# Third graph layer: one wait for landing per sixteen gathers in place of two, and its index copies moved from VectorE to ScalarE

## What is computed

```python
deg_inv_sqrt = where(deg > 0, rsqrt(deg), 0)
norm = deg_inv_sqrt[row] * deg_inv_sqrt[col]        # row, col: edges and self loops
h = x @ weight
out = segment_sum(h[row] * norm[:, None], col, num_segments=n)
return out + bias
```

## Time and profile before

| | us |
|---|---|
| median of 3 executions | 23745.33 |
| lowest and highest of the 3 | 23739.36 to 23776.59 |
| the profiled execution, its own time | 23831.74 |
| its span in the profile | 23829.8 |
| first gather of the third layer's sum, start | 13672.09 |
| last gather of it, start | 16261.36 |

### The profile page before, as it was taken

One profiled execution on the slowest core, in us unless ns is written; L12 is line 12 of the kernel. 1 busy time (PEld: TensorE's weight loads), 2 busy tenths in 40 slices (PEclk: granted clock), 3 DMA queues, 4 the chain that ended last, 5 costly groups with the idle time before them and its releaser, 6 DMA issues. The chain is left out here.

```text
span 23829.8 us, 208218 instructions
## 1 busy us (share of the span) xinstructions
PE 10305.7 (43%) x47565; PEld 6803.8 (29%) x47566; DVE 15503.2 (65%) x25810; ACT 2726.6 (11%) x6634; POOL 12726.1 (53%) x12678
## 2 busy tenths in 40 slices
PE   0033335655555555556666522221433433333333
PEld 0033332222222222222222322221333333333333
DVE  8744439998888888886666211112666666666677
ACT  0011110000000000000000000000222222222222
POOL 0188876666556565536666166663544442544543
PEclk9999995555555555558888555555555555555555
DMA  4033331111111111121111111114222222222222
GB/s 171 23 69 69 69 65 26 24 24 21 23 23 23 21 23 23 23 20 24 24 24 24 7 21 21 21 21 44 54 56 51 54 56 48 52 56 51 57 51 47
DMA packets 1151512, 957.51 MB, mean 40 GB/s; under 512 B 803964, under 2 KB 920316, under 8 KB 1150740
## 3 DMA queue, kind: packets, MB, share of 16 engines
q0 software_dynamic: 419904, 437.84, 11.2%
q1 hardware_dynamic: 730960, 512.22, 8.4%
HBM read 734.68 MB, written 210.63 MB: 40 GB/s over the span
## 5 line engine op out<-in xcount | busy, mean ns | idle before, releaser
L1451 POOL DMA_INDIRECT tail<-ball,h_idx x3328 | 3396.5, 1021 | 3961.9 <-DVEq L1761 1514.0
L737 PE MATMUL p_rad<-w_stack,hid_t 99*128 99x512 bf16 (+1 forms) x6656 | 3077.4, 619 | 2396.3 <-DVEq L827 1117.3
L809 DVE TENSOR_REDUCE red<-prod 128x96 f32<-128x1536 f32 x1664 | 2901.3, 1744 | 3.5
L1487 PE MATMUL h_sum<-head,h_hot 128*128 128x64 f32 x6656 | 1468.1, 422 | 3078.8 <-ACT head L1529 2472.1
L1101 POOL DMA_INDIRECT l_xg<-h_tab,l_idx x1664 | 1573.9, 946 | 1470.0 <-issue 958.3
L1487 PEld LDWEIGHTS h_sum<-head,h_hot 128*128 128x128 f32 x6656 | 1435.4, 332 | 3109.7 <-issue 3109.7
L338 POOL DMA_INDIRECT rec_a<-rec,slot x1600 | 1990.0, 1244 | 517.1 <-issue 510.1
L693 POOL DMA_INDIRECT rec_b<-l_rcb x1600 | 1926.1, 1204 | 570.9 <-issue 514.6
L932 POOL DMA_INDIRECT l_xg<-x_tab,l_idx x1664 | 1574.1, 946 | 1156.7 <-issue 856.8
L948 PE MATMUL l_sum<-outer,l_hot 128*128 128x512 f32 x3328 | 1671.6, 666 | 986.6 <-DVEq L993 904.8
L737 PEld LDWEIGHTS p_rad<-w_stack,hid_t 99*128 99x128 bf16 (+1 forms) x6656 | 773.4, 132 | 4338.8 <-issue 4335.4
(11 more groups left out here) (368 smaller groups left out, 18688.7 us busy)
## 6 DMA issues: line engine op xcount, KB each, us to landing
hot_t<-rows_l SPq DMA_DIRECT2D x208, 512.0 KB
rec_a<-fill SPq DMA_DIRECT2D x128, 728.0 KB, 19.5
l_rec<-rec_a SPq DMA_DIRECT2D x104, 896.0 KB, 4.8
rhot_t<-rows_r SPq DMA_DIRECT2D x208, 384.0 KB
tail<-ball,h_idx POOLq DMA_INDIRECT x3328
t<-in_type SPq DMA_DIRECT2D x100, 500.0 KB
l_xg<-in_x,l_idx POOLq DMA_INDIRECT x1664
l_xg<-x_tab,l_idx POOLq DMA_INDIRECT x1664
```

The source lines that it names most:

```text
L737: ins = pe.matmul(p_rad[j % 2][:, h * 512:(h + 1) * 512], hid_t[j // 4 % 2][0:K3 + 3 * (1 - i), j % 4, i, :], w_stack[i][0:K3 + 3 * (1 - i ...
L809: ch.step(dve.tensor_reduce(red[:, j, :], prod[j % 3][:, :, :], AX, ALU.add))
L1451: pool.indirect_dma_start(tg[q][:, j, :], None, table[:, :], bass.IndirectOffsetOnAxis(ap=idx[q][:, j:j + 1], axis=0)).then_inc(gathered[q ...
L1487: ins = pe.matmul(p_sum[:, j // 2, :], hot[j // HP8 % 2][:, j % HP8, :], hg[:, j, 0:D], start=(j % 2 == 0), stop=(j % 2 == 1))
```

## The change

GpSimd waits once per block, after its sixteenth gather. The index copies of the phase, the four at the start and the one per block, are taken from VectorE and given to ScalarE, which waits for `sum_done` by itself.

```diff
         @block.scalar
         def _(act):
             act.activation(p_row[:, 0:P], g["row"][:, :], ACT.Copy).then_inc(row_ready, 1)
+            for u in range(4):
+                act.activation(idx[u][:, :], g["src_a"][:, u * BT:(u + 1) * BT], ACT.Copy).then_inc(idx_ready, 1)
+            with act.Fori(0, NB // 4 - 1) as it:
+                for u in range(4):
+                    b = it * 4 + u
+                    hold(act, turn, sum_done, b + 1)
+                    act.activation(idx[u][:, :], g["src_a"][:, bass.ds((b + 4) * BT, BT)], ACT.Copy).then_inc(idx_ready, 1)
 
         @block.gpsimd
@@
                     for j in range(BT):
                         pool.indirect_dma_start(xg[u][:, j, :], None, table[:, :],
                                                 bass.IndirectOffsetOnAxis(ap=idx[u][:, j:j + 1], axis=0)).then_inc(gathered[u], 16)
-                        if j % 8 == 7:
-                            hold(pool, turn, gathered[u], it * (16 * BT) + 16 * (j + 1))
+                    hold(pool, turn, gathered[u], it * (16 * BT) + 16 * BT)
@@
             ch = Chain(dve, chain_s)
-            for u in range(4):
-                dve.tensor_copy(idx[u][:, :], g["src_a"][:, u * BT:(u + 1) * BT]).then_inc(idx_ready, 1)
             ch.do(dve.memset(acc[:, :, :], 0.0))
@@
                 dve.wait_ge(sum_done, b + 1)
-                if left == 2:
-                    dve.tensor_copy(idx[u][:, :], g["src_a"][:, bass.ds((b + 4) * BT, BT)]).then_inc(idx_ready, 1)
                 add_groups(dve, ch, chunk, acc, lambda k: p_sum[u % 2][:, k:k + 1, :])
```

## The result

The changed kernel takes 23611.28 us (23608.17 to 23616.38, four executions) against 23744.33 for the kernel before: a ratio of 0.9941, interval 0.9924 to 0.9959, 133 us less. The forecast was 248 less. The direction was right, the size was not.

A forecast was written before the change was run, and what follows sets the result against it. GpSimd's issue and its two landing waits were taken to bound the third layer's phase. One wait less gives 243 us in ordinary blocks and 5 in padding blocks, copies nothing: 23745.33 - 248 = 23497 us, range 23455 to 23560.

The forecast's parts named there:

- What bounds the kernel: Third layer: GpSimd's issue of sixteen gathers, 20.00 us, and two landing waits, 4.55 us, make the 24.55 us block.
- The wait taken out: Third layer: the gap before each ninth gather goes, 2.41 us in 101 ordinary blocks, 243 us; with padding blocks 248.
- the padding blocks: Last three blocks of the third layer: 31.6 us each against 33.1 now, 5 us less for the three.
- a gap of 6.85: Wait after eight gathers in padding blocks, read as a queue falling behind 0.63 us with each gather after the first.
- The index copies: Third layer: moving them from VectorE to ScalarE, 0.2 to 0.3 us each there, off the path, gives nothing.
- the cover of the index copies: Third layer: sum_done comes 7 us into block b + 1, wanted at b + 4, so some 59 us cover a 0.3 us copy.
- in ordinary blocks nothing piles up over sixteen: Third layer: sixteen gathers before one wait land as eight do, so the longer run costs nothing.
- Back pressure on issue: Rival, third layer: GpSimd stalls issuing with sixteen in flight, 104 us of the gain lost, 23601; 5%.
- The sign that I named for being wrong: Third layer: gathers longer than a microsecond, the remaining gap growing towards 4.8, or GpSimd waiting for ScalarE.
- The one-hots' hold: Rival, third layer: VectorE's 2.29 us one-hot instruction holds GpSimd's gathers, 84 us slower, 23829; 3%.
- my nearest row for the longer run: First layer's sixteen gathers with one wait behind: median 947 ns, next instruction 1.66 us after the last gather's issue ends.

The follow-up runs named there:

- e2: The changed kernel with the two landing waits per block put back, index copies still on ScalarE: 22395.71 us, 0.9998 of the kernel before.
- e1: The kernel before with one landing wait per sixteen gathers, index copies left on VectorE: 22143.18 us, 0.9885 of the kernel before.
- e3: The changed kernel, but ScalarE waits for a semaphore that VectorE raises after its own wait for sum_done: 22142.97 us, 0.9884 of the kernel before.
- f4: The kernel before without any landing wait, index copies on VectorE: 23213.82 us, 0.9925 of the kernel before.
- f3: e1 with every second tile left out of TensorE's sums, 16 matmuls per block for 32: 23168.07 us, 0.9905 of the kernel before.
- g1: e1 with GpSimd clearing 512 elements after the eighth gather and waiting for that: 23319.45 us, 0.9944 of the kernel before.
- g2: e1 with GpSimd clearing 1152 elements after the eighth gather and waiting for that: 23368.15 us, 0.9974 of the kernel before.
- f1: e1 with GpSimd clearing 2048 elements after the eighth gather and waiting for that: 23416.44 us, 1.0013 of the kernel before.
- g3: e1 with GpSimd clearing 2048 elements after the sixteenth gather, ahead of the landing wait: 23224.94 us, 0.9915 of the kernel before.

## Why the prediction missed

*What bounds the kernel.* Right. GpSimd's issue and its two landing waits were the phase; with both gone the phase is 20.0 us a block in an undisturbed sitting.

*The wait taken out.* Right in its size. Undisturbed blocks of the changed kernel take 22.05 us (13673.34 to 13695.40 is 22.06), forecast 22.2. In the undisturbed sitting the phase fell by 2579.5 - 2319.7 = 259.8 us from e2 to e1, forecast 248; the kernel before has no profile there, and e2 stands for it. (An estimate by the fixed price of a DMA in the Trainium skill, DMA: Bandwidth & Descriptors, "Anatomy of one DMA — SWDGE (gpsimd) path", had made it 216, too little.) Some 8 of the 12 us more are the padding blocks: 29.46 and 29.05 us in the changed kernel's profile, forecast 31.6. The queue falls behind by less per gather than I had read out of one gap: by the same reckoning (9.79 - 2.41) / 15 = 0.49 us for 0.63. I had also set a gap of 6.85 that holds the ordinary 0.30 against a wait of 2.41 that doesn't.

*The index copies.* 0.216 us each on ScalarE, forecast 0.2 to 0.3, and worth nothing, as forecast: e1 and e3 are equal to 0.2 us. The Trainium skill (SBUF — State Buffer, "Who interferes with whom") would have had VectorE's copies hold up GpSimd, for up to 18.5 us more; e3, which has none of them, is 0.2 us from e1, which has all. Whether the first gather comes 0.3 us later can't be told.

*The step that failed* is the cover of the index copies: "`sum_done` comes 7 us into block b + 1", so that "some 59 us" of cover remain; and, behind it, "in ordinary blocks nothing piles up over sixteen, and I cost the longer run at nothing". I looked at gathers only: their issue time, their landing. Those did hold (944 ns, at most 961). I did not ask what the longer run does to the engines beside it. In the changed kernel ScalarE's copy comes 54 us into block b + 1 in the median, and up to 69 us, in place of 7. In the blocks that GpSimd then waited for, the signal's own lateness was 37 us in the median and the matmuls took 14.5. The cover of 59 us was used up, and GpSimd waited for indices 32 times, 166.1 / 32 = 5.19 us each where a landing wait would have been 2.4: 32 x 2.8 = 90 us given back. The account closes roughly: 188 + 90 = 278, against 260 undisturbed, where the phase before was 10 us shorter to begin with (2579.5 in e2 against 2589.3). Where nothing is disturbed the step holds: e1 and e3 gain 259 us, inside the forecast's 210 to 290. Why signals come late in some sittings stays open.

*The rivals.* Back pressure on issue gave 23601, and 23611 was measured. That is luck, since its mechanism did not happen: no gather was longer than 961 ns. The sign that I named for being wrong did show: GpSimd waited for ScalarE. The one-hots' hold did not happen either; gathers kept their pitch of 1.25 us beside them.

*What stood in the profile before.* It had 299.8 us of waits at line 800 put down to "remote", a releaser that no other engine's work explained, and 274.8 us in 10 waits of ScalarE at line 713, of up to 30.3 us. Both lines are of the first layer, whose sixteen gathers in a row I had taken as my nearest row for the longer run. The fourth layer had 1737.4 us more. The third layer had none, and I took the phase by itself. That the very phase with runs of sixteen had such waits was the warning.

## To carry to other kernels

When a wait is taken out of one engine, ask what its idle time was doing for the others, and not only what follows it in the chain. Compare a change in more than one sitting, beside the kernel before: the same edit was worth 1.15% in one and 0.6 to 0.8% in others. A step that is said to be covered by three buffers is covered only as long as the signal that starts it comes at its usual time. And see whether a profile's records are complete before reading waits from them.

## What the hardware showed that I had not expected

In some sittings, while GpSimd issues gathers at 1.25 us with little rest, TensorE and VectorE go on in steps of about 0.7 us or multiples of it (matmuls 1.41 and 1.43 us apart at 13741.21, 13742.62 and 13744.05; adds 0.71 apart in f4), and signals take effect up to 53 us in the changed kernel, and 63 in f3, after the work they stand for is over by the records. In the changed kernel they recover when GpSimd stops for some 5 to 6 us. Phases with blocks of 23.56 us and more (g1, g2, f1, and 24.6 in the kernel before) have neither sign; those that would take 22.65 us or less all have late signals. Nothing between 22.65 and 23.56 was run in such a sitting. All but g3, which loses nothing, settle at 2380 to 2407 us whatever else is changed. The cause inside the chip isn't shown, nor what makes a sitting one of these: the same chip was in both. The same sittings lose landing records, and it isn't shown whether the recording is the cause. In the undisturbed ones nothing of it is seen, even with no rest at all.
